# Weight casts moved from the prologue into the chunk loop, a second weight buffer in the feed-forward stage, four decay slots in the scan

## The reference, cut to what matters

```python
x = x + _layernorm(mamba(_layernorm(x)))
x = x + _layernorm(ffn(_layernorm(x)))

# mamba: d_inner 2048, d_state 16, dt_rank 64, a causal convolution of width 4
xi, z = split(x @ W_in)                       # 1024 -> 2 x 2048
xc    = silu(conv(xi) + b_conv)
delta_lr, B, C = split(xc @ W_xproj)          # 2048 -> 64 + 16 + 16
delta = softplus(delta_lr @ W_dt + b_dt)
h_t   = exp(delta * A) * h_{t-1} + delta * B * xc     # 16 states per channel
y     = (h . C + D * xc) * silu(z) @ W_out            # 2048 -> 1024

# ffn: hidden 4096, weights are -1, 0 or 1, one scale per output channel
h = silu(x @ w1 * s1) * (x @ w2 * s2)         # 1024 -> 4096, twice
h = gelu(h @ h1 * sh1)                        # 4096 -> 4096
h = gelu(h @ h2 * sh2)                        # 4096 -> 4096
out = h @ w3 * s3                             # 4096 -> 1024
```

## Time and profile before

| what | value |
|---|---|
| median of 3 runs | 28880.06 us |
| profiled execution, its own time | 28939.05 us |
| its span (slowest core, first to last instruction) | 28936.4 us |
| spans of the 8 cores | 28816.1 to 28936.4 us |
| busy: PE, DVE, ACT | 8235.4, 12527.9, 5991.2 us |
| share of the span that is busy: PE, DVE, ACT | 28%, 43%, 21% |
| mean granted TensorE clock of the cores | 0.639 to 0.642 |

### The profile page before, as it was taken

One profiled execution on the slowest core, in us unless ns is written; L12 is line 12 of the kernel. 1 busy time (PEld: TensorE's weight loads), 2 busy tenths in 40 slices (PEclk: granted clock), 3 DMA queues, 4 the chain that ended last, 5 costly groups with the idle time before them and its releaser, 6 DMA issues.

```text
span 28936.4 us, 142918 instructions; the slowest of 8 cores (28816.1 to 28936.4 us)
## 1 busy us (share of the span) xinstructions
PE 8235.4 (28%) x23464; PEld 2536.3 (9%) x23464; DVE 12527.9 (43%) x21715; ACT 5991.2 (21%) x8281; POOL 0.2 (0%) x4
## 2 busy tenths in 40 slices
PE   0000121222222121222212122221212256565655
PEld 0000000000000000000000000000000012222222
DVE  0000647475565747465574746556474700000000
ACT  1111222222222222222222222222222200000000
POOL 0000000000000000000000000000000000000000
PEclk9999555555555555555555555555555578787878
DMA  4333000000001010100100000000001012222222
GB/s 123 115 117 97 10 32 11 32 16 27 25 16 33 10 32 12 31 25 16 34 9 32 12 30 17 25 31 11 32 11 32 15 64 73 67 71 66 70 68 70
DMA packets 823455, 1169.29 MB, mean 40 GB/s; under 512 B 448068, under 2 KB 616644, under 8 KB 786644
## 3 DMA queue, kind: packets, MB, share of 16 engines
q1 hardware_dynamic: 822548, 1160.16, 13.3%
HBM read 995.72 MB, written 164.10 MB: 40 GB/s over the span
## 4 chain that ended last, share of the span: by engine, by line
DVE 44%; PE 19%; DMA 14%; ACT 8%; issue 8%; SPq 5%; DVEq 2%; ACTq 0%
DVE sG L604 18%; PE ps L801 8%; DVE sG L600 6%; DVE sG L616 6%; DMA wwin<-wbf_h 4%; PE ps L390 4%; SPq L188 4%; DVE hcar_sb L610 2%; DVE sC L452 2%; DMA wwin<-wbf 2%; PE ps L669 2%; DMA wwin<-wbf_in 2%; DVEq L61 2%; PE ps L767 2%; ACT cast_b L247 1%
## 5 line engine op out<-in xcount | busy, mean ns | idle before, releaser
L604 DVE TENSOR_TENSOR_SCAN sG<-sGf,hcar_sb,sG 128x512 bf16<-128x512 f32 x4096 | 5256.8, 1283 | 441.3 <-DVE sG L600 18.8
L620 PE MATMUL ps<-sG,id_sb 128*128 128x512 bf16 x4096 | 2398.3, 586 | 10382.9 <-DVE sG L616 8737.2
L593 ACT ACTIVATE sGf<-sE,A_sb 128x512 f32<-128x512 f32 x4096 | 2965.0, 724 | 8721.4 <-DVE sG L604 8011.6
L297 DVE TENSOR_SCALAR ps<-ps 1x512 f32<-1x512 f32 x52 | 35.7, 686 | 6008.0 <-PE ps L292 6008.0
L600 DVE TENSOR_TENSOR sG<-sF,bcb 128x512 bf16<-128x512 bf16 x4096 | 1741.0, 425 | 599.0 <-DMA bcb<-bc_dr 160.3
L616 DVE TENSOR_TENSOR sG<-sG,bcb 128x512 bf16<-128x512 bf16 x4096 | 1743.6, 426 | 456.6 <-DVE hcar_sb L610 39.4
L620 PEld LDWEIGHTS ps<-sG,id_sb 128*128 128x128 bf16 x4096 | 425.3, 104 | 12368.5 <-issue 12368.5
L801 PE MATMUL ps<-fb,wwin 128*128 128x512 bf16 x4096 | 1144.8, 449 | 690.4 <-DMA wwin<-wbf_h 690.4
L390 PE MATMUL ps<-bA,wwin 128*128 128x512 bf16 x4096 | 1118.5, 441 | 780.1 <-DMA wwin<-wbf_in 569.3
L801 PE MATMUL ps<-fa,wwin 128*128 128x512 bf16 x4096 | 1138.1, 447 | 692.2 <-DMA wwin<-wbf_h 692.2
L285 PE MATMUL ps<-bX,ones_sb 128*1 128x512 bf16 x336 | 196.4, 584 | 3962.4 <-ACT bQ L281 3962.4
(11 more groups left out here) (91 smaller groups left out, 7429.8 us busy)
## 6 DMA issues: line engine op xcount, KB each, us to landing
wwin<-wbf_h SPq DMA_DIRECT2D x512, 512.0 KB, 4.5
wwin<-wbf_in SPq DMA_DIRECT2D x128, 1024.0 KB, 4.8
bcb<-bc_dr SPq DMA_DIRECT2D x1024, 128.0 KB, 4.0
cast_f<-h1t SPq DMA_DIRECT2D x32, 2048.0 KB, 7.9
wbf_h<-cast_b SPq DMA_DIRECT2D x2048, 32.0 KB, 1.6
cast_f<-h2t SPq DMA_DIRECT2D x32, 2048.0 KB, 7.9
sA<-x_seq SPq DMA_DIRECT2D x32, 2048.0 KB, 9.5
wwin<-wbf_out SPq DMA_DIRECT2D x64, 1024.0 KB, 4.8
```

What stands on the lines that cost most here:

```text
L593: e.activation(out=da, in_=sE[:, s], func=AF.Exp, scale=A_sb[:, ti * NST + n: ti * NST + n + 1]))
L604: e.tensor_tensor_scan(out=hh, data0=da, data1=dbx, initial=hcar_sb[:, ti * NST + n: ti * NST + n + 1], op0=ALU.mult, op1=ALU.add))
L620: yp_pe[it] = pem(lambda e, yp=yp, j=j, n=n: e.matmul(out=ps[j][:, 0:T], lhsT=id_sb[:], rhs=yp, start=(n == 0), stop=(n == NST - 1)))
```

## The change

The change has four parts.

- Casts. The prologue keeps the casts of W_in and W_out. The other five weights are cast in smaller steps (`make_cast_step`): a load of 128 x 1024 float32 into a new buffer `cstg_f`, an ACT copy to `cstg_b`, and 8 stores of 128 x 128. There are 352 steps (32 + 32 + 128 + 128 + 32). Each chunk runs 22 of them, between the W_in block and the convolution.
- Feed-forward weights. A second buffer `wwinF` is added. Odd m use it, even m use `wwin`. SP waits ahead of a load for the last matmul that read this buffer, two tiles back.
- Scan. `sGf` has four slots, and the exp of iteration `it` waits for scan `it - 4`.
- Memory. `bC` becomes another name of `bI`; ACT waits for the W_out matmuls of the chunk before ahead of the W_in block.

```diff
+        cstg_f = sb("cstg_f", [128, 1024])
+        cstg_b = sb("cstg_b", [128, 1024], BF16)
...
-            cast_tiled(w1_in, wbf_1, KT, HT, 1, 128)
-            cast_tiled(w2_in, wbf_2, KT, HT, 1, 128)
-            cast_tiled(h1_in, wbf_h1, HT, HT, 1, 128)
-            cast_tiled(h2_in, wbf_h2, HT, HT, 1, 128)
-            cast_tiled(w3_in, wbf_3, HT, KT, 1, 128)
             p.barrier()
...
+        def make_cast_step(srcw, dst, k, c0, ncols, slab_m):
+            def step():
+                p.wait("sync", "sAC", cast_state["tc"])
+                tl = ld(cstg_f[:, 0:ncols],
+                        srcw[k * 128:(k + 1) * 128, c0:c0 + ncols])
+                p.wait("scalar", "sLD", tl)
+                for tok in cast_state.get("sts", []):
+                    p.wait("scalar", tok)
+                tc = ac(lambda e: e.copy(out=cstg_b[:, 0:ncols],
+                                         in_=cstg_f[:, 0:ncols]))
+                cast_state["tc"] = tc
+                p.wait("sync", "sAC", tc)
+                w = slab_m * 128
+                sts = []
+                for mb in range(c0 // w, (c0 + ncols) // w):
+                    sts.append(st(dst[mb * 128:(mb + 1) * 128,
+                                      k * w:(k + 1) * w],
+                                  cstg_b[:, mb * w - c0:(mb + 1) * w - c0]))
+                cast_state["sts"] = sts
+            return step
...
-            sGf = msb("sGf", [128, 2 * T])
+            sGf = msb("sGf", [128, 4 * T])
...
-            bC = msb("bC", [128, NT * T], BF16)
+            bC = bI
...
                 if "td_conv" in edges:
                     p.wait("scalar", "sDV", edges["td_conv"])
+                if "tp_wout" in edges:
+                    p.wait("scalar", "sPE", edges["tp_wout"])
...
                 edges["tp_win"] = tp
+                nsteps = (len(cast_steps) + NCH - 1 - c) // (NCH - c) \
+                    if c < NCH else 0
+                for _ in range(min(nsteps, len(cast_steps))):
+                    cast_steps.pop(0)()
                 p.wait("vector", "sAC")
...
-                            if it >= 2:
-                                p.wait("scalar", "sDV", scan_done[it - 2])
+                            if it >= 4:
+                                p.wait("scalar", "sDV", scan_done[it - 4])
...
                 def hlayer(wsrc, scol, src, dst):
+                    win_tp = fwin_tp
                     for m in range(HT):
-                        toks = [ld(wwin[:, kb * 2048:(kb + 1) * 2048],
+                        win = wwin if m % 2 == 0 else wwinF
+                        p.wait("sync", "sPE", win_tp[m % 2])
+                        toks = [ld(win[:, kb * 2048:(kb + 1) * 2048],
...
+                        win_tp[m % 2] = tp
                         p.wait("scalar", "sPE", tp)
...
                         p.wait("tensor", "sAC", ta)
-                        p.wait("sync", "sPE", tp)
```

More of the change, by code:

```diff
@@ L269, in build_program @@
         p.barrier()
+        cast_steps = []
+        cast_state = {"tc": 0}
+        def make_cast_step(srcw, dst, k, c0, ncols, slab_m):
[14 more added lines that the diff above has]
+                    sts.append(st(dst[mb * 128:(mb + 1) * 128,
+                                      k * w:(k + 1) * w],
+                                  cstg_b[:, mb * w - c0:(mb + 1) * w - c0]))
+                cast_state["sts"] = sts
+            return step
+        for (srcw, dst, krows, mcols) in (
+                (w1_in, wbf_1, KT, HT), (w2_in, wbf_2, KT, HT),
+                (h1_in, wbf_h1, HT, HT), (h2_in, wbf_h2, HT, HT),
+                (w3_in, wbf_3, HT, KT)):
+            for k in range(krows):
+                for c0 in range(0, mcols * 128, 1024):
+                    nc_ = min(1024, mcols * 128 - c0)
+                    cast_steps.append(make_cast_step(srcw, dst, k, c0, nc_, 1))
         def layer_norm2(v, out_bf, xb, qb):
@@ L582, in build_program @@
                             it = n * HHT + j
-                            da = sGf[:, (it % 2) * T:(it % 2 + 1) * T]
+                            da = sGf[:, (it % 4) * T:(it % 4 + 1) * T]
                             dbx = sG[:, 0 * T:1 * T]
@@ L731, in build_program @@
             fss = fsb("fss", [128, T])
+            wwinF = fsb("wwinF", [128, 4096], BF16)
             scal_sb = fsb("scal_sb", [128, 4 * HT + KT])
+            fwin_tp = {0: 0, 1: 0}
             ld(scal_sb[:, 0:HT], s1_in)
@@ L766, in build_program @@
                     for k in range(KT):
-                        f = (lambda e, k=k: e.matmul(
+                        f = (lambda e, k=k, win=win: e.matmul(
                             out=ps[0][:, 0:T],
-                            lhsT=wwin[:, k * 128:(k + 1) * 128],
+                            lhsT=win[:, k * 128:(k + 1) * 128],
                             rhs=flb[:, k * T:(k + 1) * T],
@@ L773, in build_program @@
                     for k in range(KT):
-                        f = (lambda e, k=k: e.matmul(
+                        f = (lambda e, k=k, win=win: e.matmul(
                             out=ps[1][:, 0:T],
-                            lhsT=wwin[:, 2048 + k * 128:2048 + (k + 1) * 128],
+                            lhsT=win[:, 2048 + k * 128:2048 + (k + 1) * 128],
                             rhs=flb[:, k * T:(k + 1) * T],
```

10 lines of the change are left out of this document (4 added, 6 removed).

## The result

| what | before | after |
|---|---|---|
| median, same chip | 28881.0 us (8 runs) | 27582.62 us (8 runs, 27523.49 to 27771.73) |
| ratio | | 0.9555, 95% interval 0.9535 to 0.9575 |
| profiled execution, its own time | 28939.05 us | 27558.04 us |
| its span | 28936.4 us | 27555.8 us |
| busy: PE, DVE, ACT | 8235.4, 12527.9, 5991.2 us | 7513.9, 12527.8, 6021.0 us |

The kernel became 4.45% faster.

What follows compares the result with a forecast made beforehand. No single engine bounds it: a serial cast chain limits the prologue, DVE the chunks, PE's weight waits the feed-forward stage. 28,936 - 2,469 + 3,114 - 2,352 = 27,229 us span, 27,170 us median; range 27,000 to 27,850, own range 27,030 to 27,380.

Steps and rivals of the forecast that it cites:

- prologue ends: Prologue: the memset that ended it at 2759.77 us would come at about 291.1 us.
- casts in a chunk: Between W_in and convolution: 22 steps of 9.15 us add 194.6 us a chunk, 3,114 us in 16.
- saved in an h or w3 tile: Feed-forward: an h tile falls from 14.33 to 8.13 us, saving 6.20; 256 h and 32 w3 tiles save 1,786 us.
- saved in a w1/w2 tile: Feed-forward: a w1/w2 tile falls from 10.1 to 5.6 us, saving 4.5; 128 tiles save 576 us.
- table loads: Feed-forward: 8 activation table loads of 1.3 us on ACT, until now under the load wait, cost about 10 us.
- Part 1: Prologue: taking casts out removes 2,469 us.
- Part 2: Chunks: 22 cast steps in each, hidden by nothing, add 3,114 us in 16 chunks.
- rival 2: Chunk casts: 4 KB row pieces could double the 3.6 us load, adding 1,270 us, 28,440 us in all; chance 11%.
- Part 3: Feed-forward stage: two weight buffers cover the load and the clock stays at the upper level, 2,352 us less.
- Part 4: Scan and memory: four decay slots and bC on bI gain 0; the extra ACT wait costs 0.05 us a chunk.
- Rival 1: Feed-forward clock doesn't hold: at mean 0.83 a matmul takes 0.259 us, Part 3 gives 1,875, time 27,650 us; chance 30%.
- Rival 3: Feed-forward PE stays at the lower clock: Part 3 gives 50 us, time 29,470; break-even mean clock 0.58; chance 4%.

Runs made afterwards that it cites:

- e2: Kernel before with the casts moved into the chunk loop and bC on bI, one weight buffer, two decay slots: 29474.36 us, ratio 1.0227.
- e4: Changed kernel with ACT's 8 waits for the old stores put ahead of its wait for the load: 27449.6 us, ratio 0.9522.
- e5: Changed kernel with the 352 cast steps put beside the scan, one per state and half, load issued one state ahead: 24477.86 us, ratio 0.849.
- e1: Kernel before with only the second feed-forward weight buffer and its waits, all casts still in the prologue: 26904.19 us, ratio 0.9345.
- e6: Changed kernel with two PSUM banks (two pairs in w1/w2) for successive feed-forward tiles: 26820.23 us, ratio 0.9321.
- e10: Changed kernel where PE in w1/w2 waits for this tile's silu and the product of two tiles back: 27363.58 us, ratio 0.9479.
- e7: Changed kernel with two w1/w2 tiles in one buffer, so 32 matmuls without a gap: 27398.9 us, ratio 0.9514.
- e3: Kernel before with only four decay slots of sGf and bC on bI: 28825.61 us, ratio 0.9999.
- e8: Changed kernel with the spread casts of e5 and the two PSUM banks of e6 together: 23680.0 us, ratio 0.8222.
- e11: e8 with the feed-forward activations set to zero behind their load, every load, matmul and wait kept: 23557.0 us, ratio 0.8161.

## Why the prediction was right, and where it was off

The sum of the prediction was 27,229 us of span. Its terms, for the slowest core of the profiled execution:

| term | forecast | measured | difference |
|---|---|---|---|
| prologue ends | 291.1 | 279.7 us | -11 |
| casts in a chunk | 194.6 | 197.4 us, x 16 | +45 |
| saved in an h or w3 tile | 6.20 | 5.94 us, x 288 | +76 |
| saved in a w1/w2 tile | 4.5 | 3.11 us, x 128 | +178 |
| table loads | 10 us back | in the two rows above | -10 |
| wait for B and C | 0 | see below | +59 |
| sum | 27,229 | 27,566, against a span of 27,555.8 | +337 |

The savings are taken from the starts of the stretches in the timelines of both kernels: a w1/w2 tile went from 9.98 to 6.87 us, an h or w3 tile from 14.25 to 8.31.

*Part 1* was right. *Part 2* was right in mechanism and size: nothing hid the casts (e2: +650 against +645), 8 satisfied waits cost about 0.5 us where 0.4 was taken (e4), and the strided load cost nothing more (3.6 us), which ends rival 2. The first steps keep 9.0 us apart and the mean is 9.3, up to 9.5 on other cores. In e4, which passes the store waits during the load, steps are 8.7 to 8.9 us apart, near the 8.74 of the w3 casts, so most of the excess is what the waits cost. The profile of e5 shows how completely the place in the lists decided.

*Part 3* holds the step that failed: the clock over the new gaps in w1/w2. Its words were: "The new gaps of 1.08 and 2.0 us are shorter than those 3.4 us, so I take the upper level for the whole stage." For the h layers that held on this core. For w1/w2 it did not: the term of 576 us was mis-sized and came out at 398, since a tile's 16 matmuls take 4.7 us in the mean and not 3.61. e1 shows that the loss comes with the second weight buffer, e6 and e10 that it is the clock and goes with the gap (378 ns with no gap and 382 with 1.5 us, instead of 504), e7 that twice the burst with a gap of 2.4 us still falls. The evidence of the earlier trace rows misled: the three tiles in a row at 1.00 over gaps of 3.4 us were the only ones of this core's 128 that took 3.6 us; all others took 4.9 us or more, and no other core had more than 7 such tiles. The means were at hand: 0.83 in a window over the h layers, and 6.35 us of matmuls in a w1/w2 tile (6.2 without the overlap of the two groups). 6.2 - 3.6 = 2.6 us of slow clock in a mean tile would have warned. The smaller miss, 0.2 us in each h tile, is the handover from ACT to PE, taken as 0.24 us with the load waits and measured as 0.35, and the first tile of each layer.

*Part 4* was right at zero (e3), on its own. e5 kept the four slots; whether its copies would have been hidden with two was not tried.

*Rival 1* was half there. As priced (s = 0.259 us in every matmul of the stage) it is wrong: s was (7.10 - 0.38)/31 = 0.217 in the h layers and (4.7 - 0.38)/15 = 0.288 in w1/w2, and the latter is a mixture of tiles at the two usual levels and no third one. But the third level exists. Windows of the changed kernel, cores 6 and 5, of the same die, in the last block's h layers:

```profile
27000.00:27200.00 200.00, 170.86 (x775) 74.03 (x774) 0.00 (x0) 16.50 (x24) 0.00 (x0) 1.00 0.39 129
```

```profile
27000.00:27200.00 200.00, 173.53 (x705) 71.26 (x704) 0.00 (x0) 15.17 (x22) 0.00 (x0) 0.89 0.36 116
```

Core 5 spent six tenths of this window at 0.81 and the rest at 1.00. Core 4 went with it, while cores 6 and 7 kept 1.00 in their h layers; on the other die cores 2 and 3 had 0.81 for 120 us of h1 in this block and cores 0 and 1 never. This did not set the end of the profiled execution (core 1 did), but other runs went up to 27,772 us, and in e8 one die ended 250 us after the other. The Trainium skill ("TensorE: Matmul & The Clock Gate", Part 1) names a limiter that takes a die to 13/16, and says that it depends on the data. The traces agree in the level (0.81), and e11 speaks for the data. They disagree on the unit, which here was a pair of cores (0 and 1, 2 and 3, 4 and 5, 6 and 7) and not always the die, and on how regularly it comes: all eight cores ran dense matmuls, and in e8 the h layers of cores 4 and 5 stayed at 1.00.

That the time lies in the wide range is owed to the part of it that was opened for rival 1: the clock did fall, but in w1/w2 alone and as a mixture of the two usual levels, which is not what rival 1 described.

*Rival 3* (lower level throughout) did not come, but its break-even was sound: e2 shows that the trade of the prologue alone loses, so part 3 carries the gain.

*The wait for B and C* is new. Ahead of the product with B, DVE waited 160.3 us for `bcb` before and 219.6 us after on core 1:

```profile
L635 DVE TENSOR_TENSOR sG<-sF,bcb 128x512 bf16<-128x512 bf16 x4096 | 1741.0, 425 | 658.3 <-DMA bcb<-bc_dr 219.6
```

Only cores 0 and 1 show it (201.6 and 219.6 us); the other cores wait 162 to 167 us, and before all eight waited 160 to 163. Why those two was not tried and stays open.

The forecast missed the median by 413 us. Of these, 327 are span (27,555.8 against 27,229); the other 86 are the step from span to median, where the forecast took off 59 us as before had it, and after's median stands 27 us above its profiled span. That lies in the spread of after's 8 runs, 248 us.
